# A transformer decoder layer on one core: scaling of each norm in a step of its own, closing norms as a work stream, first loads in another order

## The reference

```python
x = _layernorm(x + attention(x, Wqkv, Wo))          # 16 heads of 128, 2 kv heads, rotary, causal, soft-capped
x = _layernorm(x + cross_attention(x, ctx, mask))   # 16 heads of 16, W8A8 linear in and out
x = _layernorm(x + ffn(x, Wr, br, W1, W2))          # 16 blocks of 64, the 4 best per token, exact GELU

def _layernorm(x, axis=-1, eps=1e-05):
    m = jnp.mean(x, axis=axis, keepdims=True)
    v = jnp.var(x, axis=axis, keepdims=True)
    return (x - m) / jnp.sqrt(v + eps)
```

## Time and profile before

| what | value |
|---|---|
| device time, median of 3 | 392.63 us (392.15 to 393.03) |
| the profiled execution, its own time | 394.29 us |
| its span in the profile | 392.5 us |
| PE busy | 374.3 us (95%) |
| DVE busy | 295.0 us (75%) |
| ACT busy | 231.3 us (59%) |
| POOL busy | 148.3 us (38%) |

### The profile page before, as it was taken

One profiled execution on the slowest core, in us unless ns is written; L12 is line 12 of the kernel. 1 busy time (PEld: TensorE's weight loads), 2 busy tenths in 40 slices (PEclk: granted clock), 3 DMA queues, 4 the chain that ended last, 5 costly groups with the idle time before them and its releaser, 6 DMA issues.

```text
span 392.5 us, 8974 instructions
## 1 busy us (share of the span) xinstructions
PE 374.3 (95%) x3038; PEld 316.6 (81%) x3038; DVE 295.0 (75%) x900; ACT 231.3 (59%) x492; POOL 148.3 (38%) x172
## 2 busy tenths in 40 slices
PE   6999999999999999989999999999999999899893
PEld 5778898788898968768998777898878787679783
DVE  2898888576669858888897788888888677887603
ACT  1568654455648865366387854758783266884230
POOL 5697844838443243444433231542112321000101
PEclk9999999999999999999999999999999999999899
DMA  7991744733334333314443131031202000000000
GB/s 268 368 335 56 251 153 145 214 98 109 109 124 117 111 82 82 80 56 133 135 128 90 55 80 29 28 121 42 83 28 86 24 3 13 15 3 2 27 3 27
DMA packets 21404, 38.42 MB, mean 98 GB/s; under 512 B 2544, under 2 KB 12144, under 8 KB 21360
## 3 DMA queue, kind: packets, MB, share of 16 engines
q1 hardware_dynamic: 20272, 36.80, 30.3%
q10 hardware_dynamic: 1088, 1.05, 0.8%
HBM read 25.52 MB, written 5.24 MB: 78 GB/s over the span
## 4 chain that ended last, share of the span: by engine, by line
PE 76%; DVE 7%; DMA 5%; POOL 4%; issue 4%; ACT 2%; SPq 1%; POOLq 0%; DVEq 0%; ACTq 0%
PE acc L587 10%; PE bank L481 8%; PE bank L672 7%; PE bank L531 6%; PE bank L733 6%; PE bank L554 6%; PE bank L753 5%; PE bank L684 4%; DMA rope_s<-rope_t 3%; PE bank L568 3%; PE bank L557 3%; PE bank L661 3%; PE bank L539 3%; PE bank L613 2%; PE bank L650 2%
## 5 line engine op out<-in xcount | busy, mean ns | idle before, releaser
L911 ACT ACTIVATE xs<-xs,xneg 128x256 f32<-128x256 f32 x128 | 53.7, 497 | 18.2 <-DVE xneg L1188 18.2
L1355 POOL TENSOR_TENSOR a_lo<-a_flat,a_hi 128x512 fp32r<-128x512 f32 x32 | 41.6, 1302 | 37.4 <-ACT a_flat L830 37.4
L1344 POOL TENSOR_TENSOR q_T<-q_T,rope_s 128x512 f32<-128x512 f32 x24 | 31.2, 1302 | 56.3 <-DMA rope_s<-rope_t 56.1
L587 PE MATMUL acc<-wo_s,a_hi 128*128 128x256 f32 x256 | 50.6, 296 | 0.9 <-POOL a_lo L1355 0.9
L1373 POOL TENSOR_TENSOR small<-small,half 128x1 f32<-128x1 f32 x24 | 13.2, 550 | 95.2 <-DVE small L1074 95.2
L1188 DVE CUSTOM_DVE_ANT_0 xs<-bank,mask_s 128x256 f32<-128x256 f32 x128 | 45.7, 419 | 2.4 <-PE bank L661 2.4
L587 PEld LDWEIGHTS acc<-wo_s,a_hi 128*128 128x128 f32 x256 | 39.4, 189 | 4.0 <-issue 1.9
L554 PE MATMUL bank<-v_s,p_near 128*128 128x129 f32 x256 | 40.6, 276 | 0.2 <-POOL p_far L1362 0.2
L830 ACT CAST a_hi<-bank 128x512 fp32r<-128x512 f32 x32 | 18.8, 586 | 33.9 <-PE bank L568 33.7
L554 PEld LDWEIGHTS bank<-v_s,p_near 128*128 128x128 f32 x256 | 34.9, 191 | 4.1 <-issue 3.9
L481 PE MATMUL bank<-x_hi,wqkv_hi 128*128 128x256 f32 x124 | 38.0, 307 | 0.0
(11 more groups left out here) (168 smaller groups left out, 959.5 us busy)
## 6 DMA issues: line engine op xcount, KB each, us to landing
wo_s<-wo_parts SPq DMA_DIRECT2D x24, 512.0 KB, 3.3
rope_s<-rope_t SPq DMA_DIRECT2D x54, 128.0 KB, 2.3
wo_parts<-wo_s SPq DMA_DIRECT2D x8, 512.0 KB, 3.0
xs<-in_wo SPq DMA_DIRECT2D x8, 256.0 KB, 5.8
stage<-in_wqkv SPq DMA_DIRECT2D x2, 512.0 KB, 6.7
xp_T<-in_wqkv SPq DMA_DIRECT2D x2, 512.0 KB, 8.4
y<-in_x SPq DMA_DIRECT2D x4, 256.0 KB, 2.7
ctx_s<-in_ctxT SPq DMA_DIRECT2D x4, 256.0 KB, 3.5
```

The source lines that it names most:

```text
L587: ins = mm(acc[:, t, :], a[x], wo_s[:, slot, w, m, :], start=(j == 0 and t == 0 and m == 0 and p == 0), stop=(j == PAIRS - 1 and m == 1 an ...
L911: activation(xs[:, t, m, m2, :], xs[:, t, m, m2, :], ACT.Exp, bias=xneg[:, t, m, m2:m2 + 1], scale=-1.0)\
L1344: g.tensor_tensor(dst, dst, (rope_s if b else rope_t)[:, n % 2], ALU.add).then_inc(sig["rotated", 0], 1)
L1355: g.tensor_tensor(a_lo[:, j % 2], a_flat[:, j % 2], a_hi[:, j % 2].bitcast(F32), ALU.subtract)\
```

## The change

1. `layer_norm` ends with the eps step. The wait for POOL and the scaling are a function `scale` and stand in operations of their own: `scale1`, `scale2`, `scale3`. In streams m and o the statistics of both tiles come first and then both scalings; in x and y `scale2` follows `outproj`.
2. The third norm leaves `ffn`/`last` and becomes `norm3` and `scale3` in a new stream o (`close_ops`). The store of the output goes with `scale3`.
3. `ORDER` is another string with 563 letters in place of 531 (24 scalings and 8 `norm3` more). All operations of PE are the same ones, with other neighbours.
4. SP's first loads: `raw[1]` comes directly behind `xT_s`, ahead of the tables; the v half of `raw[0]` moves from ACT's queue to SP's, behind the tables.
5. In the first letters `val` now stands ahead of `split_x` and `piece`.

```diff
-    return [(kind, b, i, 0) for kind, i in ops] + [("norm1", b, 0, t) for t in range(TT)]
+    return [(kind, b, i, 0) for kind, i in ops] + [(kind, b, 0, t) for kind in ("norm1", "scale1") for t in range(TT)]
...
-    ops += [("turn_o", 0), ("quant_o", 0), ("turn_ox", 0), ("outproj", 0)]
+    ops += [("turn_o", 0), ("quant_o", 0), ("turn_ox", 0), ("outproj", 0), ("scale2", 0)]
...
+def close_ops(b):
+
+    return [(kind, b, 0, t) for kind in ("norm3", "scale3") for t in range(TT)]
...
 ORDER = (
-    "rrrrrmsmrmssrrmrsrmmmmrsssmrmmmsrsmmmmmrrmmmmmmmmmrsssmmcmmrmmccmmmmrrcccmcccmmrrcsssmmmmmccrmmsrcssxmmmr"
+    "rrrmrrsmrmssrmrrsrmmmmrsssmmrmrmssmmmmmrrmmmmmmrmmmsssmcmmrrccmmmrmmcmcccmcccmmmssrrmccsmmmcmmmrsmxmmmssr"
...
+            "o": [op for b in every for op in close_ops(b)],
...
             sp.dma_start(xT_s[:], rows(xT[0])).then_inc(x_in, 16)
+            sp.dma_start(raw[1], rows(wqkv[:, 0:PW])).then_inc(piece_in[1], 16)
             sp.dma_start(cos_s[:], cos).then_inc(tables_in, 16)
             sp.dma_start(sin_s[:], sin).then_inc(tables_in, 16)
-            for n in range(1, PIECES):
+            sp.dma_start(raw[0][:, :, PAIR:PW], rows(wqkv[:, NH * HD + PAIR:])).then_inc(values_in, 16)
+            for n in range(2, PIECES):
                 sp.dma_start(raw[n], rows(wqkv[:, (n - 1) * PW:n * PW])).then_inc(piece_in[n], 16)
...
-                elif kind == ("last" if b == B - 1 else "ffn"):
+                elif kind == "scale3":
                     wait_for(sp, "ln3", b, 4, t)
...
-            act.dma_start(raw[0][:, :, PAIR:PW], rows[:, :, NH * HD + PAIR:]).then_inc(values_in, 16)
...
-            def layer_norm(n, b, t, do, done, h, y):
+            def layer_norm(n, t, do, done, h):
...
                 do(v.tensor_scalar(var_eps[n][:, t:t + 1], moments[n][:, t, 1:2], EPS_LN, None, ALU.add))
-                wait_for(dve, f"rstd{n + 1}", b, 0, t)
-                do(v.tensor_scalar(y[:, t, :], h[:, t, :], moments[n][:, t, 0:1], rstd[n][:, t:t + 1],
-                                   ALU.subtract, ALU.mult))
+
+            def scale(n, b, t, h, y):
+                wait_for(dve, f"rstd{n}", b, 0, t)
+                v.tensor_scalar(y[:, t, :], h[:, t, :], moments[n - 1][:, t, 0:1], rstd[n - 1][:, t:t + 1],
+                                ALU.subtract, ALU.mult).then_inc(sig[f"ln{n}", t], 1)
...
+                layer_norm(1, t, do, done, q_tmp)
+
+            def scale2(b, t):
                 wait_filled(dve, "turn_z", b - 2)
                 wait_for(dve, "ln3", b - 2, 0, t)
-                layer_norm(1, b, t, do, done, q_tmp, z[b % 2])
+                scale(2, b, t, q_tmp, z[b % 2])
...
-            def ffn(b, t):
+            def norm3(b, t):
                 wait_for(dve, "last", b, 0, t)
...
-                layer_norm(2, b, t, do, done, y3, y3)
+                layer_norm(2, t, do, done, y3)
...
-                elif kind == ("last" if b == B - 1 else "ffn"):
+                elif kind == "norm3":
                     inverse_root(2, b, "ln3", 3, t)
```

More of the change, by code:

```diff
@@ L147 @@
 ORDER = (
-    "rrrrrmsmrmssrrmrsrmmmmrsssmrmmmsrsmmmmmrrmmmmmmmmmrsssmmcmmrmmccmmmmrrcccmcccmmrrcsssmmmmmccrmmsrcssxmmmr"
[L149 to L153, removed]
+    "rrrmrrsmrmssrmrrsrmmmmrsssmmrmrmssmmmmmrrmmmmmmrmmmsssmcmmrrccmmmrmmcmcccmcccmmmssrrmccsmmmcmmmrsmxmmmssr"
+    "mmrsmmrxsmmmsmmymcmrmmmyxsymssryxmmyxrymmmxxxrryyyxxmmmmsyyxmmxxysyyxymxmmmymmxxysxyrxyxyrrmxyyxmmxysmxxs"
+    "smmrmccmxmmxysssccxxymmmmrrmmyxccmymmxsymssyxmmmnyxmmymmmrxxxmymmyxrxnxxyxymyyxrmyxsxyxmmrxyysxysyxymryym"
+    "myysrmxyyxmmnxysxxyynrnxccsyxrxxncccnmmmxysmcsyxnxmmyyoxxymsxmmmymxxynyyoyxymmrnyoxyxxyyyxxmyyxxyysxxymmy"
+    "xxyxyonxysxsxyymcmmmmmmxnmmyxmmycymmmnmmxmnncycccyxnyxxnxoyxynonxyyxyyoxyyyxxyyxxxyyyoxxxyyxxxyyyxxxnyxyx"
+    "nnnnxxyynxyxynnnnnnnnnnnnnnnoononooooo")
 def work_streams():
@@ L1084, in norm1 @@
                 do(v.tensor_tensor(h[:, t, :], acc[:, t, :], h[:, t, :], ALU.add))
-                layer_norm(0, b, t, do, done, h, h)
+                layer_norm(0, t, do, done, h)
             def quantise(src, do, done, tiles):
@@ L1283, in _ @@
                     norm1(b, t)
+                elif kind == "scale1":
+                    scale(1, b, t, y1[:, b % 2], y1[:, b % 2])
+                elif kind == "scale2":
+                    scale2(b, t)
+                elif kind == "scale3":
+                    scale(3, b, t, y3, y3)
                 elif kind == "quant_w":
@@ L1309, in _ @@
                     router(b)
-                elif kind == ("last" if b == B - 1 else "ffn"):
-                    ffn(b, t)
+                elif kind == "norm3":
+                    norm3(b, t)
         @block.gpsimd
```

## The result

The changed kernel took 383.82 us (median of 6, 382.99 to 385.79), the kernel before 392.83 beside it (392.15 to 395.2): ratio 0.977, 95% interval 0.9741 to 0.98, a gain of 9.0 us. The forecast was 386.9, the bottom of its range 384.0. The profiled execution of the changed kernel took 384.47 in all, 9.8 less than the profiled one of before (394.29).

The account below looks back on a forecast made before the run. PE was taken as the bound, busy 374.3 of 392.5 us, its idle time mostly at the ends. Gains 1.3 + 1.4 + 1.3 + 0.7 + 1.0 = 5.7 off the median 392.63 gave 386.9, likeliest case's range 384.0 to 388.3.

Parts of the forecast that it names:

- First loads: Start of the kernel: raw[1] lands at 7.0, first scores come earlier; gain 1.3 us, from 0.8 to 1.8.
- The middle: From 10 to 310 us, scalings and new order: gain 1.4 us, at most the 3.9 that PE idles there.
- the three located waits: In the middle, three waits of PE (0.83, 1.15, 0.93) lose their cause in the new order: 2.9 us gained.
- the 1.5 set against them: In the middle, 1.5 us taken off for waits that a new order makes where none were.
- SP's stores: Stores move with scale3, so SP no longer stands ahead of swaps and weight loads; no gain counted.
- Batch 3's cross attention: Start of batch 3's cross attention: first exponential earlier, gain carried through the ACT-bound stage; 1.3 us, bounds 0.3 and 2.0.
- The last network: Batch 3's last network: z_lo no longer behind batch 2's third norm; gain 0.7 us, bounds 0 and 0.7.
- The last norm: End of the kernel: tile 0 scaled while POOL does tile 1; gain 1.0 us, bounds 0.7 and 1.1.
- Table loads: ACT: ten loads where it had eight, 1.28 us each, counted as hidden; rival that they show, 391.9, 5%.
- The low clock: Around 370 to 380 us: granted clock 0.83 follows PE's idle time; left as it is, no gain counted.
- the middle did not give its gain back: Rival for the middle: PE waits for other things instead, no gain to 3 us lost; 388.3 up to 391.3, 25%.
- Both tiles in step: Slower rival, cross attention of batches 0 and 2: eight exponentials in a row hold PE, 4.0 lost each; 393.4, 7%.

Follow-up runs that it names:

- e3: The kernel before with only the new order of the first loads; 392.53 us, ratio 0.9977 to the kernel before.
- e4: The changed kernel with the first loads in the old order; 385.0 us, ratio 0.9778 to the kernel before.
- e13: New list for the first 253 of 563 operations with the new first loads, list of before from there; 390.58 us, ratio 0.9921 to the kernel before.
- e11: The kernel before with four operations moved so that three waits of PE lose their cause; 392.42 us, ratio 0.9978 to the kernel before.
- e1: The kernel before, list and loads kept, with each scaling put two operations behind its statistics; 392.35 us, ratio 0.9966 to the kernel before.
- e2: The changed kernel with every scaling directly behind its own statistics again; 401.61 us, ratio 1.0196 to the kernel before.
- e10: The changed kernel with SP's output stores at the third norm's statistics instead of its scaling; 390.1 us, ratio 0.9915 to the kernel before.
- e16: List and loads of the kernel before up to operation 474, the new list from there; 390.67 us, ratio 0.9934 to the kernel before.
- e14: New list for the first 474 operations with the new first loads, list of before from there; 386.93 us, ratio 0.9831 to the kernel before.
- e8: The changed kernel with norm3 and scale3 of batch 2 back ahead of turn_z of batch 3; 385.08 us, ratio 0.9791 to the kernel before.
- e9: The changed kernel with one far score moved ahead of batch 0's hidden parts, 8 table loads not 10; 385.11 us, ratio 0.9792 to the kernel before.
- e15: List and loads of the kernel before, but operations 254 to 474 in the new list; 394.05 us, ratio 1.0004 to the kernel before.
- e5: The changed kernel with only the first norm's scalings directly behind their own statistics; 393.08 us, ratio 0.999 to the kernel before.
- e6: The changed kernel with only the second norm's scalings directly behind their own statistics; 390.56 us, ratio 0.9911 to the kernel before.

## Why the prediction was too small

*First loads*, 1.3 forecast: 0.9 in the traces at the first scores, 0.9 by `e3`, 0.3 by `e4`. The mechanism was right (one piece, DVE's second rotation at 9.70, inside the 8.8 to 9.8 forecast), though the load landed at 5.9, not 7.0: from there PE and its clock were the limit, not the load. DVE's first rotation came later, as forecast. The first scores came at 13.23, not near 12.8; where the clock rose early they stood at 12.54 (`e13`).

*The middle*, 1.4 forecast: 4.2 (2.0 and 2.2 in the table). This is the step that failed, in three of its parts. First, "PE has only 3.9 us to gain from it": that bound was taken from PE's idle time, though neighbouring matmuls overlap in the records (before, the third rotation's matmuls end at 12.27 and `val` begins at 12.11), so that short waits don't show. The 384.0 at the bottom of the range came from it and the start's 1.8. Against 3.9 shown, PE had by the sum above waited some 13.45 us between the first scores and `proj` 7 of batch 3, and waits 9.28 now. The same in stretches, to the place of exchange and from it to the third; first before, then after:

```profile
10.00:184.30 174.30, 171.35 (x1300) 143.30 (x1299) 139.26 (x348) 105.79 (x211) 94.49 (x98) 1.00 0.47 145
184.30:322.00 137.70, 135.72 (x1220) 116.39 (x1218) 111.50 (x382) 88.88 (x200) 43.70 (x50) 1.00 0.24 70
```

```profile
10.00:181.60 171.60, 169.30 (x1295) 142.33 (x1294) 138.85 (x353) 105.21 (x210) 97.89 (x98) 1.00 0.48 149
181.60:316.40 134.80, 134.02 (x1218) 116.25 (x1217) 110.57 (x379) 92.47 (x204) 43.53 (x50) 1.00 0.24 68
```

Idle fell by 0.65 and 1.20, the stretches by 2.7 and 2.9; of these 5.6, 0.9 are the start's. Second, the three located waits, 2.9: taken away by themselves they gave 0.9 (`e11`). Third, the 1.5 set against them for waits that a new order makes: the new ones are there (0.65 and 0.48 shown above), but by the same sum the waits under 0.3 us fell by some 2.3 us in all, and the net has the other sign. Splitting the scalings in the old order gives 1.3 over the whole kernel (`e1`), of which its trace has 1.0 in the last norm, so little of the 4.2; and the new order without the split is 7.7 slower than before (`e2`). What the two do together is shown; which neighbours in the list remove the short waits stays open.

*SP's stores*, "I count nothing": for the old order this rests on its trace, where no wait of PE hung on them, and was not tested. In the new one their place is worth 5.7 (`e10`). The prediction looked for PE's waits behind the stores in the trace of before, and a trace of the old order can't show what the new order leans on.

*Batch 3's cross attention*, 1.3 forecast, with 2.0 as its upper bound: from `proj` 7 on 1.8, of which 0.6 come ahead of the first `xscore` and 1.2 inside the stage. The 0.33 us ahead of the first exponential went as forecast; PE then followed it more closely than before (0.68 idle in the stage instead of 1.37). `e16` and the step from `e14` to the changed kernel put everything from the queries of batch 3 to the end at 2.6 and 2.4.

*The last network*, 0.7: 0.7, and `e8`'s trace gives 0.73. *The last norm*, 1.0: 0.97. Both were right. *Table loads*, nothing: `e9` agrees.

*The low clock*, "follows PE's idle time; I leave it as it is": 1.3 of the profiled pair, and it does not follow the wait for `z_lo` alone. With the wait as it was (0.85 to 0.86) `e11` and `e15` had the stretch, `e3` and `e13` had none; `e16`, where the new order had cut this wait to 0.18, had it, and `e8` with 0.96 had none. So it comes and goes, and what starts it stays open. The medians (9.0) probably hold less of it than the profiles (9.8): over 79 executions of the kernel before, the 32 with a mean granted clock of 0.997 or more have a median of 392.75, the others one of 394.06.

The rivals: the middle did not give its gain back; the table loads did not show. "Both tiles in step" was wrong for the changed kernel, where PE has no new wait of over 1 us. It was near in kind: `e5` and `e10` lose 8.6 and 5.7 us with one cover missing, and `e2`, with all three norms joined, is slower than before.

## What to carry to other kernels

Idle time of an engine whose records overlap is no upper bound for what a new order can give (here 3.9 shown and 4.2 gained, while the idle time itself fell by 1.6): take its start times against the plain sum of its work. An order and the places of the short waiting steps (a scaling behind another engine's result, a store in a queue with loads) have no separate prices; test them together and each one taken away. To find where a new order earns, exchange it piecewise where both lists hold the same set, and look at the handover before taking a piece's result for its worth.

## What had not been expected of the hardware

After one wait of PE of 3.42 us (`e5`) its granted clock stood at 0.50, the lower of its two levels, for 3.4 us, after 1.76 (`e15`) likewise, and around those of 4.32 (`e10`) and 3.40 (`e2`) for 6.8 us; so these waits cost more than their length. The length alone does not decide it: after 1.96 (`e6`) and 2.55 (`e2`, at 330.28) no such stretch followed, and near 370 us it came behind waits of 0.82 and 0.18 (`e16`). The changed kernel's profile has no such stretch between the start and the end of its work.

The first full clock came at 4.4 us in `e13` and at 8.7 in `e2`, with the same loads and the same first operations of PE, and their first scores stood at 12.54 and 14.48. So some 2 us of the start are not in the kernel's hand in a single profile. The Trainium skill, TensorE: Matmul & The Clock Gate, Part 1: The HAM clock gate, says that the low clock is the default state and that activity releases it, and calls the slow start run-variable; these two runs agree.
